# Attention of a two-layer kernel: two phases a batch instead of four, and the next rows placed elsewhere

## What is computed

```python
q = proj(query, Wq, bq)
k = proj(key, Wk, bk)
v = proj(value, Wv, bv)
scale = 1.0 / jnp.sqrt(jnp.float32(hd))
scores = jnp.einsum('bhqd,bhkd->bhqk', q, k) * scale
scores = scores + mask * -1000000000.0
attn = jax.nn.softmax(scores, axis=-1)
ctx = jnp.einsum('bhqk,bhkd->bhqd', attn, v)
ctx = ctx.transpose(0, 2, 1, 3).reshape(b, s, d)
return jnp.einsum('bsd,ed->bse', ctx, Wo) + bo
```

## Time and profile before

| | us |
|---|---|
| median of 3 runs | 757.78 |
| lowest, highest | 757.25, 758.8 |
| profiled execution | 756.75 |
| its span, first to last instruction | 755.0 |
| attention, batch 0 to 14 (turned score to turned score) | 336.6 to 512.3 |
| last batch, and up to tile_norm | 512.3 to 525.1 |

### The profile page before, as it was taken

One profiled execution on the slowest core, in us unless ns is written; L12 is line 12 of the kernel. 1 busy time (PEld: TensorE's weight loads), 2 busy tenths in 40 slices (PEclk: granted clock), 3 DMA queues, 4 the chain that ended last, 5 costly groups with the idle time before them and its releaser, 6 DMA issues.

```text
span 755.0 us, 14956 instructions
## 1 busy us (share of the span) xinstructions
PE 573.7 (76%) x4495; PEld 408.0 (54%) x4496; DVE 521.2 (69%) x1445; ACT 390.3 (52%) x739; POOL 214.9 (28%) x243
## 2 busy tenths in 40 slices
PE   5399999169999999658889788886417766676575
PEld 3288888069998989435555454453103343334334
DVE  6278876856665566644456676663478989989997
ACT  1344442033343433255557566566668768867672
POOL 5626763525665456411103333210000000000000
PEclk9699999679999999879999999997667878988978
DMA  8773442396666555160000000000000000000001
GB/s 319 246 227 116 149 139 88 118 354 224 198 190 222 187 180 181 41 210 2 1 0 0 0 0 0 0 2 1 4 0 0 14 28 14 29 14 28 14 28 56
DMA packets 35535, 68.42 MB, mean 91 GB/s; under 512 B 5581, under 2 KB 24542, under 8 KB 34464
## 3 DMA queue, kind: packets, MB, share of 16 engines
q1 hardware_dynamic: 28816, 52.37, 21.3%
q0 software_dynamic: 5520, 13.61, 5.2%
q10 hardware_dynamic: 1152, 1.88, 0.8%
HBM read 53.78 MB, written 15.80 MB: 92 GB/s over the span
## 4 chain that ended last, share of the span: by engine, by line
PE 46%; DVE 19%; ACT 15%; issue 8%; DMA 6%; SPq 3%; POOL 2%; DVEq 0%; ACTq 0%; POOLq 0%
PE quad L1113 9%; PE quad L1178 4%; PE bank L1187 4%; PE quad L1460 3%; PE duo L1303 2%; DVE nM L2060 2%; ACT nPT L866 2%; PE quad L1469 2%; PE bank L1495 2%; ACT hqT L1012 2%; PE quad L1292 2%; PE bank L1249 2%; DMA x_after_ffn<-row,niU 2%; DMA early<-in_W 2%; ACT ctxs L995 2%
## 5 line engine op out<-in xcount | busy, mean ns | idle before, releaser
L776 ACT ACTIVATE hid<-quad,early 128x128 f32<-128x128 f32 x156 | 44.6, 369 | 82.6 <-PE quad L1178 82.6
L1178 PE MATMUL quad<-xts,early 128*128 128x128 f32 x624 | 74.4, 278 | 3.7 <-DMA early<-in_W 3.6
L1178 PEld LDWEIGHTS quad<-xts,early 128*128 128x128 f32 x624 | 72.8, 194 | 5.9 <-issue 4.1
L1187 PE MATMUL bank<-W2s,hid 128*128 x312 | 70.5, 379 | 0.0
L2060 DVE TENSOR_REDUCE nM<-quad 128x16 f32<-128x1024 f32 x32 | 39.1, 1221 | 38.2 <-PE quad L1269 38.2
L1187 PEld LDWEIGHTS bank<-W2s,hid 128*128 128x128 f32 x312 | 57.8, 190 | 7.1
L597 POOL DMA_INDIRECT x_after_ffn<-row,niU x39 | 39.0, 1000 | 56.5 <-DVE row L1845 40.1
L2217 DVE SCALAR_TENSOR_TENSOR hh<-quad,gmx,sil 128x512 f32<-128x512 f32 x64 | 45.2, 745 | 13.6 <-PE quad L1469 6.8
L1316 PE MATMUL bank<-WoS,nC 128*128 128x256 f32 x128 | 39.0, 430 | 15.8 <-DVE nC L2074 15.0
L1840 DVE SCALAR_TENSOR_TENSOR row<-bank,sco,row 128x256 f32<-128x256 f32 x39 | 18.6, 476 | 45.0 <-PE bank L1187 44.5
L983 ACT ACTIVATE sil<-quad,gmx 128x512 f32<-128x512 f32 x64 | 41.0, 689 | 13.4 <-PE quad L1460 9.5
(11 more groups left out here) (359 smaller groups left out, 1339.1 us busy)
## 6 DMA issues: line engine op xcount, KB each, us to landing
early<-in_W SPq DMA_DIRECT2D x37, 514.0 KB, 5.6
row<-rows_by_expert SPq DMA_DIRECT2D x38, 134.0 KB, 2.2
early<-in_ctxO SPq DMA_DIRECT2D x4, 1024.0 KB, 7.8
ctxs<-in_ctxT SPq DMA_DIRECT2D x4, 1024.0 KB, 13.7
W2s<-in_W SPq DMA_DIRECT2D x8, 512.0 KB, 3.7
X<-x_after_ffn SPq DMA_DIRECT2D x7, 516.0 KB, 6.9
out<-yo SPq DMA_DIRECT2D x14, 256.0 KB, 2.1
early<-in_W ACTq DMA_DIRECT2D x2, 514.0 KB, 8.3
```

Of the source, the lines that this page charges most:

```text
L776: ins = act.activation(hid[:, u, c * P:(c + 1) * P], bank[2 + u][:, c * P:(c + 1) * P], ACT.Gelu, bias=W1r[:, k, DC * H2 + c:DC * H2 + c + 1])
L1178: ins = pe.matmul(bank[2 + u][:, n * P:(n + 1) * P], W1r[:, m % RING, c * H2 + n * P:c * H2 + (n + 1) * P], xt[:, u, c, :], start=c == 0, ...
L1187: ins = pe.matmul(bank[6 + u % 2][:, 0:D], hid[:, u, c * P:(c + 1) * P], W2s[:, bass.ds(ex, 1), c, :].rearrange("p o s -> p (o s)"), start ...
```

## The change

A batch is done in two phases. quad is used whole for one thing at a time: score computes both halves q and signals once, row_max reduces all 2048 columns in one instruction, score_turned computes both halves c and signals once, and one exponential of 2048 columns makes nPT. The score of b + 1 now waits until the exponential of b is done. project computes both halves into the two halves of bank 7, and add_rows adds both in one instruction. maxima_turn goes to bank 7 instead of bank 0. weigh is still in two parts but waits once.

On TensorE the order within a batch is: turned score, projection of b - 1, the next rows' transposes, score of b + 1, both weighings, half of the queries, maxima_turn, the other half. On ScalarE: queries_out before the exponential, rows_norm right behind rows_out, weight_half before inverse_sums. On VectorE: the weights' piece first, then add_rows(b - 1), row_max, maxima, new_stats, and the division last. In the last batches done_roots(0) is moved ahead of batch 15, with a load of the exponential's table behind it.

```diff
-        nPT = [sb(f"nPT{c}", [P, 4, S], F32, en) for c in range(DC)]
+        nPT = sb("nPT", [P, 4, DC * S], F32, en)
...
-        scored, keyed = quad[:, :, 0:S], quad[:, :, S:2 * S]
+        by_half = [quad[:, :, n * S:(n + 1) * S] for n in range(2)]
...
 (ScalarE)
-                def exps(b, c):
-                    act.wait_ge(n_ST, b * 2 + (c + 1))
-                    act.activation(nPT[c][:], keyed, ACT.Exp, bias=keym[:, 0:1]).then_inc(n_exp, 1)
+                def exps(b):
+                    act.wait_ge(n_ST, b + 1)
+                    act.activation(nPT[:], quad[:], ACT.Exp, bias=keym[:, 0:1]).then_inc(n_exp, 1)
...
                 def batch(b, h, p=None, first=False, k=None, stage=0):
-                    exps(b, 0)
                     if stage < 2:
                         queries_out(b + 1, 1 - h)
-                    exps(b, 1)
+                    exps(b)
                     if stage == 0:
                         rows_out(b + 2)
-                    else:
-                        weights_out(0 if stage == 1 else 3)
+                    if stage == 0 and b is not NB - 3:
+                        rows_norm(b + 3)
                     if stage < 2:
                         values_in(p, b + 1, 1 - h, first)
-                    if stage == 0 and b is not NB - 3:
-                        rows_norm(b + 3)
-                    if stage:
-                        weights_out(1 if stage == 1 else 4)
-                    inverse_sums(b)
                     if k is not None:
                         weight_half(k, first=isinstance(k, int) and k == 0)
+                    if stage == 1:
+                        weights_out(0)
+                    inverse_sums(b)
+                    if stage:
+                        weights_out(1 if stage == 1 else 3)
                     if stage < 2:
                         maxima_out(b + 1)
...
                 batch(NB - 2, 0, p=NB // 2 - 1, stage=1)
+                done_roots(0)
+                act.preload_act_table_set("natural_log_exp_and_others")
                 batch(NB - 1, 1, stage=2)
-                done_roots(0)
...
 (TensorE)
+                def score(b, h, first=False):
+
+                    pe.wait_ge(n_qe, b + 1)
+                    pe.wait_ge(n_kb, b + 1)
+                    if not first:
+                        pe.wait_ge(n_exp, b)
+                    for q in range(2):
+                        scored = by_half[q]
...
+                def score_turned(b, h):
+
+                    pe.wait_ge(n_mTe, b + 1)
+                    for c in range(DC):
+                        keyed = by_half[c]
...
+                def project(b):
+                    pe.wait_ge(n_cn, b + 1)
+                    pe.wait_ge(n_ad, b)
+                    for q in range(2):
+                        for k in range(DC):
+                            ins = pe.matmul(bank[7][:, q * D:(q + 1) * D], nC[:, k, q * P:(q + 1) * P], WoS[:, k, :], start=k == 0, stop=k == DC - 1)
                     ins.then_inc(n_wo, 1)
...
 (VectorE)
-                def row_max(b, q):
-
-                    v.wait_ge(n_S, b * 2 + (q + 1))
-                    red(nM[:, q, :].rearrange("p (k m) -> p k m", k=4), scored.rearrange("p k (m s) -> p k m s", m=4),
+                def row_max(b):
+
+                    v.wait_ge(n_S, b + 1)
+                    red(nM[:].rearrange("p k q m -> p k (q m)"), quad[:].rearrange("p k (n s) -> p k n s", s=KW),
                         AX.X, ALU.max).then_inc(n_rd, 1)
...
                 def batch(b, first=False, between=None):
-                    if not first:
-                        add_rows(b - 1, 1)
-                        new_stats(b - 1, 1)
                     if between:
                         between()
-                    row_max(b + 1, 0)
-                    row_max(b + 1, 1)
+                    if not first:
+                        add_rows(b - 1)
+                    row_max(b + 1)
+                    maxima(b + 1)
+                    if not first:
+                        new_stats(b - 1)
                     divide(b)
-                    maxima(b + 1)
-                    add_rows(b, 0)
-                    new_stats(b, 0)
```

162 lines of the change are left out of this document (69 added, 93 removed).

## The result

The changed kernel takes **732.0 us**, the median of 4 runs (731.03 to 732.55), against 758.29 for the kernel before beside it (757.25 to 758.93). The ratio is 0.9653, with a 95% interval of 0.9636 to 0.967. The direction is the forecast one. The profiled execution took 732.55, its span is 730.3.

What follows compares the result with a forecast made beforehand. No engine full, TensorE nearest, its waits to be won. Batch gains of 16.9 us, less 3.2 at the end and 0.5 behind tile_norm, gave 13.2: 743.5 profiled, 744.6 us median; range 738 to 750.

Steps and rivals of the forecast that it cites:

- The waits: TensorE in plain batches: waits of 0.89 (division), 0.54 (nMT) and 0.17 us (exponential) go; 0.4 on nMb stays.
- TensorE's groups: Plain batch summed from earlier-trace matmul prices, such as 0.66 per half turned score: 10.1 us against 11.4.
- The rival that something in the chain would be dearer: Serial exponential, score and maximum: 0.5 us more in each of 15 batches, 752.1 us; chance 0.13.
- The hold by GpSimd: Batches 5 to 11: weight_scaled holds steps of maxima, TensorE waits 1.3 us, batch 11.0 us against 11.9.
- The rival that GpSimd misses maxima: weight_half later or hold released sooner: seven weight batches take 10.1 us each, total 738.2; chance 0.1.
- The exponential: ScalarE's one exponential of 2048 columns: 2.17 us, covered by 0.4 us of projection and transposes.
- The maximum: VectorE's 2048-wide maximum, on the path: 2.29 us taken, between 2.13 and 2.44.
- Batch 0: First batch, 12.85 us before: 10.9 with the score at half clock, 9.8 at full clock; gain 1.9.
- The end: Last turned score to tile_norm: 16.0 us against 12.77, 2.4 us of table loads and root bare; loss 3.2.
- The clock rival: Stops lower TensorE's clock: 755.8 us if in the seven weight batches, 768.6 if in all fifteen; chance 0.04.
- Between tile_norm and x_in: VectorE behind tile_norm does a double add_rows and two bn_stats where half stood: 0.5 us more.
- cover of the exponential: Projection and transposes ahead of the score on TensorE keep it from waiting for the exponential, by 0.4 us.

Runs made afterwards that it cites:

- e2: Changed kernel with the halves of the turned score and of the projection alternating, seven changes of matmul kind a batch in place of five; 745.18 us.
- e5: Changed kernel with the next rows' transposes (rows_in) put back behind the first half's weighing; 745.31 us.
- e10: Changed kernel with one extra 64-column matmul on 32 rows between the projection's halves, its result never read; 738.51 us.
- e11: Changed kernel with one extra 64-column matmul on all 128 rows between the projection's halves, its result never read; 736.0 us.
- e12: e5's kernel with ScalarE's copy of nMT (maxima_out) moved ahead of inverse_sums; 735.09 us.
- e3: Changed kernel with ScalarE's weight_half put back behind inverse_sums; 727.26 us.
- e6: Changed kernel with square roots as exp(0.5 ln(v)), needing no other table, the first root behind the last exponential; 728.81 us.
- e1: Changed kernel with four already satisfied waits a batch, ahead of second halves of turned score, projection, score and weighing; 733.12 us.
- e9: Changed kernel with e3's and e6's edits, plus half of the second query projection moved ahead of the maxima's turn; 720.74 us.

## Why the prediction was right in direction and wrong in size

**The waits: right.** The division's wait, the wait on nMT and the one on the exponential are gone, 0.38 on nMb is left (0.4 forecast), and the score is not held by the exponential. The projection has no wait.

**TensorE's groups: the step that failed.** The batch was summed from prices in the earlier trace rows such as 0.66 for half a turned score and 1.06 for half a projection, as if they added up. They are prices of a group that is followed, and mostly also preceded, by another kind. In their new places they cost less: ahead of the score 0.47 (360.47 + 0.53 = 361.00, 3.56 behind the turned score against 4.03 counted), within the score up to the maximum 0.11, behind the turn of the maxima 0.14. With 0.07 less on VectorE this is the 0.79 between 10.09 and 9.30. A change of kind costs 0.10 to 0.16 by e2, e5, e10, e11 and e12; the rows of the changed kernel alone give 0.09 or 0.10, the half of a score, a turned score or a weighing ahead of another kind against the one ahead of its own. Of the ten changes before, two stood where TensorE stopped anyway, for 0.54 and 0.17 us. So eight lay bare and five do now: three fewer explain 0.3 to 0.5 of TensorE's 0.9. The two stops fewer (three before, one now) explain some 0.3 more by the rows, though no experiment separates this. A stop is listed from the end of the last matmul on, and a matmul's end lies behind the place where a next one of its kind would have started: half a projection counts 1.13 ahead of a stop (361.57 in the earlier trace rows), but 0.97 ahead of its own kind. The 0.97 is from the row at 370.54 in the earlier trace rows to this one:

```profile
371.51 0.27 PE L1279 MATMUL duo<-identb,nMb 128*128 128x128 bf16 x2
```

The remaining 0.1 to 0.3 are not tied to a cause. These rows of before could have shown the step's fault: 0.97 ahead of the same kind, 1.06 ahead of another. In the sum the term is worth 3.2 us in batches 1 to 4, 2.0 in batches 12 to 14 and 7 x 0.79 = 5.5 in batches 5 to 11, of which 4.1 show, since the hold cost more than counted. With these 9.3 us added to 732.0 the time would lie inside the range. The rival that something in the chain would be dearer had a chance of 0.13, and that the groups would be cheaper had none. That is why the range ended at 738.

**The hold by GpSimd: right.** The first cast and L2063 are stretched in batches 5 to 11, the wait is 1.46 (1.3 forecast), and those batches take 10.41, 1.11 more than a plain one (0.9 forecast). The two stretched steps are 0.62 and 0.46 us longer than in e3, together 1.08 of the 1.11, and e3, where they run free, has none of the 1.11: this is the hold. The rival that GpSimd misses maxima did not come about in the changed kernel; it is what e3 makes.

The Trainium skill's page "SBUF — State Buffer", section "SBUF: two separate sides", says that VectorE and GpSimd share a port pair as an exclusive lock, for VectorE operations in a two-port mode or, against a GpSimd operation that reads SBUF, with two SBUF inputs, and that the loser waits for the whole operation. The traces agree with it: L2063, which has two SBUF inputs, is held until 414.79, 0.05 behind GpSimd's end (413.01 + 1.73), while a maximum, which reads PSUM, kept its 1.22 us wholly beneath a GpSimd operation before. In the changed kernel the two overlap by 0.12 to 0.44 us only, so its 2.29 tests this little.

**The exponential: mis-sized, without effect.** 1.97 us and not 2.17. The forecast took 0.53 for each further 512 elements from a copy's length; by the exponential itself 1024 elements more cost 1.97 - 1.11 = 0.86. It has cover. The maximum is 2.29 as taken.

**Batch 0**: 10.25 against 10.9. Half clock did occur there, but over the turned score and the transposes and not over the score. In e3 and e6, whose batch 0 has the same code, it lay over the score, as was taken, and batch 0 took 10.75 and 10.76. The same code, run again, had full clock throughout the batch and took 9.19. The first two rows are from the changed kernel's profile, the other two from that run:

```profile
331.68 1.99 PE L1251 MATMUL bank<-xt,WqS 128*128 128x256 f32 x8 [0.68 <-ACT xt L851]
...
338.08 1.06 PE L1293 MATMUL quad<-nQT,nKB 32*128 32x256 f32 x8
```

```profile
333.69 3.75 PE L1251 MATMUL bank<-xt,WqS 128*128 128x256 f32 x8 [0.68 <-ACT xt L851]
...
338.42 0.61 PE L1293 MATMUL quad<-nQT,nKB 32*128 32x256 f32 x8
```

TensorE had stood 3.81 us before the turned score in the first run, waiting for nMT, and 0.75 in the second. The short stop is itself an effect of the clock: in the second run the half clock fell earlier, on the eight matmuls of the query projection ahead of the stage (3.75 us instead of 1.99), and they filled most of the wait. nMT came at nearly the same time in both (turned score at 337.89 and 338.30). So the term depends on which matmuls meet the half clock, and that differs from run to run; what sets it is not shown.

**The end: mis-sized by 2.0.** tile_norm came 13.98 behind the last turned score, where the range was 13.8 to 16.7 and 16.0 was taken. The two table loads do lie bare ahead of the exponential, but the weighing behind the 2.87 us stop ran at full clock. In e3 behind a stop of 2.88 it ran at half clock, and the distance was 15.59. The other kernels with this tail fall on either side: 13.98 or 13.99 in e1, in e10 and in the changed kernel run again, 15.46 to 15.63 in e2, e5, e11 and e12. So the case that was taken, 16.0, exists but for 0.4 us, and the rows available did not tell which one applies.

**The clock rival** did not come about. The clock stayed at 1.00 over stops of 0.38 us in plain batches and some 1.5 in those with weight work. The Trainium skill's page cited with it, "TensorE: Matmul & The Clock Gate", section "A second HAM failure mode: psum-queue depth-cycling", would have such stops swing the clock; the trace does not agree, 1.00 from 395 to 468 us.

**Altogether.** 0.65 + 3.2 + 4.1 + 2.0 in the batches and 2.0 at the end make 11.95. Between tile_norm and x_in (at 512.92) 12.01 us pass (12.19 before; 0.5 more was forecast): 0.7 more. The work behind x_in is 0.3 shorter. The first turned score was 1.3 later (337.89 against 336.58), and 0.5 more lies outside the span. The sum is 11.1, against 743.5 - 732.55 = 10.95 for the profiled executions.

**Which part carries the gain.** Without the new place of the transposes 14.7 of the 26 us are gone (e5), by the queue on ScalarE above all. The place is one way to keep that queue from being late and not the only one: in e12 the transposes are late too, only the copy of nMT goes ahead, and the stage from the first to the last turned score takes 149.2 us, close to the changed kernel's 149.0 and 148.0, though in part because the hold by GpSimd is gone there. The prediction counted them only as cover of the exponential, and they are not needed for that: in e5 the score starts as early without them. What they do, letting ScalarE go on directly behind the exponential, was not seen; the forecast of the waits held without it, because in the new order ScalarE stands only 0.36 us for the transposes and the copy of nMT is not late.

## What to carry to other kernels

Price a group of matmuls by what stands next to it: halves of one tiling kind put together saved 0.1 to 0.16 us here at each bare change that went, while waits that are satisfied cost nothing that shows. When a step is moved on one engine, follow the engine that reads it: an in-order queue that stands for a late input delays everything behind it, and in e5 that cost more than the two added changes of kind. Once the waits are single and known, a piece of independent work of the same kind moved from behind the wait to ahead of it takes away what is left of it (e9).

## What the runs showed of the hardware that was not expected

- A change between matmuls on 128 rows and on 32 rows or 32 columns costs TensorE 0.11 us (e10 against e11) to 0.16 (e2), at full clock.
- A wait that is already satisfied costs TensorE nothing that shows: four more a batch, 9.30 us with and without (e1).
- A stop costs more than the idle time listed for it: half a projection counts 1.13 us ahead of a stop and 0.97 ahead of a matmul of its own kind.
- A further small matmul of 64 columns costs 0.11 us on the path within a run of the same kind (e11), though it starts only 0.03 ahead of the next one.
- Behind a stop of 2.87 us the eight matmuls of the weighing ran at full clock in one kernel, and behind 2.88 at half clock in another (e3), after the same instructions on TensorE. At the start of the stage the clock differed even between two runs of the same code: half clock lay over the query projection ahead of the stage in one (3.75 us for 1.99) and over the first turned score in the other.
